# RWKV stage of a two-layer block: the routing's last step and the row transfers behind the third group instead of the fourth

## The reference

```python
xk = x * time_mix_k + x_prev * (1.0 - time_mix_k)      # same for xv, xr
k = xk @ W_k.T; v = xv @ W_v.T; r = sigmoid(xr @ W_r.T)
y = r * wkv_scan(k, v, decay, first)                   # over 2048 tokens, per channel
attn = y @ W_o.T

router_probs = softmax(x @ router)                     # 8 experts
topk_probs, topk_idx = top_k(router_probs, 2)
routed = sum over the two experts of topk_probs * expert(x)
ffn = routed + shared_expert(x)
```

## Time and profile before

| | us |
|---|---|
| median of 3 runs | 1508.13 (1507.18 to 1508.47) |
| the profiled execution, its own time | 1510.13 |
| its span | 1508.4 |
| RWKV stage in it | 1106.7 to 1295.8 |
| MoE stage in it | 1295.8 to 1508.4 |
| VectorE busy in 1109 to 1295.8 | 161.1 of 186.8 |
| TensorE busy there | 134.5 |
| ScalarE busy there | 119.2 |
| GpSimd busy there | 69.6 |

### The profile page before, as it was taken

How to read it: one execution, slowest core, us unless ns; L and a number is a source line. 1 busy time by engine, 2 the same in 40 slices (tenths; PEclk the granted TensorE clock), 3 DMA queues, 4 the chain that set the end, 5 groups by cost and what they waited for, 6 DMA issues and landing times. The chain is left out here.

```text
span 1508.4 us, 27417 instructions
## 1 busy us (share of the span) xinstructions
PE 1316.8 (87%) x9558; PEld 596.6 (40%) x9558; DVE 1272.9 (84%) x2268; ACT 998.8 (66%) x1316; POOL 324.4 (22%) x574
## 2 busy tenths in 40 slices
PE   4776999999999999999999986999767767689987
PEld 2454223232232332323322212766633334377754
DVE  6896999999999999999999933799868999665668
ACT  3452355888888888888888886666358665356642
POOL 3220000110102111020110202323100177300475
PEclk9897688999999999999999998999979889899999
DMA  6887312141423404242043024596372155686776
GB/s 206 269 257 219 57 33 45 20 81 29 83 46 41 85 7 79 46 79 49 11 76 74 12 48 116 169 315 198 136 232 86 56 171 184 215 253 205 229 227 194
DMA packets 158521, 186.16 MB, mean 123 GB/s; under 512 B 18228, under 2 KB 134708, under 8 KB 157364
## 3 DMA queue, kind: packets, MB, share of 16 engines
q1 hardware_dynamic: 135384, 151.45, 37.6%
q0 software_dynamic: 6144, 16.79, 3.6%
q10 hardware_dynamic: 16864, 16.26, 3.1%
HBM read 100.81 MB, written 83.36 MB: 122 GB/s over the span
## 5 line engine op out<-in xcount | busy, mean ns | idle before, releaser
L1334 DVE TENSOR_REDUCE att_m_part<-att_mx 128x1 f32<-128x512 f32 (+3 forms) x1152 | 680.8, 653 | 30.1 <-PE att_mx L1402 14.2
L1364 ACT ACTIVATE att_prob<-att_score,late_score_scale 128x1024 f32<-128x1024 f32 (+3 forms) x640 | 595.1, 986 | 167.2 <-PE att_score L1441 165.1
L1402 PE MATMUL att_mx<-early_kop,early_qop 48*128 48x512 f16 (+3 forms) x1280 | 354.6, 367 | 22.8 <-DVE att_m_part L1334 5.6
L1424 PE MATMUL att_pv<-att_prob,early_v 128*32 128x512 f32 (+3 forms) x2560 | 305.6, 550 | 2.0 <-POOL att_prob L1301 2.0
L1441 PE MATMUL att_score<-early_qop,early_kop 50*128 50x512 f16 (+3 forms) x1280 | 253.4, 358 | 10.3 <-ACT att_prob L1364 9.3
L1301 POOL TENSOR_SCALAR_AFFINE_SELECT att_prob<-att_prob 128x256 f32<-128x256 f32 x256 | 102.7, 406 | 671.4 <-ACT att_prob L1364 670.6
L1402 PEld LDWEIGHTS att_mx<-early_kop,early_qop 48*128 48x128 f16 x1280 | 98.5, 94 | 374.4 <-DVE att_m_part L1334 347.0
L2241 PE MATMUL rwkv_prod<-rwkv_xm,late_mixT 128*128 128x512 f32 x192 | 100.3, 675 | 37.1 <-ACT rwkv_kvr L2195 27.4
L1441 PEld LDWEIGHTS att_score<-early_qop,early_kop 50*128 50x128 f16 x1280 | 72.1, 94 | 72.5 <-ACT att_prob L1364 56.4
L1990 POOL DMA_INDIRECT rows<-rwkv_xs,routing_slot_i x64 | 69.6, 1087 | 112.2 <-DVE routing_slot_i L2082 93.0
L2462 POOL DMA_INDIRECT moe_yg<-results,routing_slot_i x64 | 64.6, 1009 | 128.6 <-issue 126.1
(11 more groups left out here) (264 smaller groups left out, 1752.9 us busy)
## 6 DMA issues: line engine op xcount, KB each, us to landing
va<-qkv_v SPq DMA_DIRECT2D x8, 1024.0 KB, 6.7
early_v<-va SPq DMA_DIRECT2D x8, 1024.0 KB, 7.5
moe_xt<-rows SPq DMA_DIRECT2D x30, 256.0 KB, 3.7
rows<-att_zeros SPq DMA_DIRECT2D x8, 928.0 KB, 6.5
early_kop<-qk SPq DMA_DIRECT2D x48, 128.0 KB, 4.4
routing_xp<-parts SPq DMA_DIRECT2D x24, 256.0 KB, 3.7
results<-moe_y ACTq DMA_DIRECT2D x24, 256.0 KB, 2.9
results<-blend_x ACTq DMA_DIRECT2D x22, 256.0 KB, 2.7
```

The lines of the kernel that those rows point to most:

```text
L1334: nc.vector.tensor_reduce(cells[:, sides[0]:sides[-1] + 1, some], mx[:, banks[0]:banks[-1] + 1, 0:len(hps) * w].rearrange("p a (h w) -> p ...
L1364: nc.scalar.activation(prob[:, r % (PROBS * HP), :, n0:], score[:, r % 2, :, n0:], ACT.Exp, scale=late_weights.score_scale[:, 0:1])\
L1402: op = nc.tensor.matmul(bank[:, n * w:(n + 1) * w], qop[rows, slot, t, hp, i * P:(i + 1) * P], kop[rows, slot, hp, c * GT:c * GT + w], sta ...
L1424: op = nc.tensor.matmul(pv[at, n0:], v[:, slot, j, at], prob[:, (st * HP + h // 2) % (PROBS * HP), h % 2, n0:], start=(j == 0), stop=(j == ...
```

## The change

The constant ROUTED of the RWKV stage goes from 4 to 3. It stands in the steps of VectorE, ScalarE, TensorE and SyncE, so all that is tied to it is done one step sooner: `below_top` in step 1, `choice`, the exponential and the count in step 2, `places` in step 3, the loads of chunks 2 and 3, 4 and 5, 6 and 7 in steps 5, 6 and 7. GpSimd's program is the same; its transfers wait for `places`.

```diff
@@ -1827,7 +1827,7 @@
     HALVES = TG * C // GT
     XP = 2
     CHUNKS = NT // TG
-    ROUTED = 4
+    ROUTED = 3
     wT, mix, unmix = late_weights.mixT, late_weights.mix, late_weights.unmix
```

## The result

The changed kernel takes 1513.65 us (median of 7 runs, 1512.43 to 1517.39) where the kernel before takes 1510.13 (7 runs, 1507.18 to 1510.70): ratio 1.0034, 95% interval 1.0021 to 1.0047, which is some 5.1 us slower (0.0034 of 1510). The ratio rests on all runs: the two medians alone lie 3.5 us apart, the two means 5.0. A second set of runs gave 1.0031 (1.0017 to 1.0046). The forecast was 8.9 us slower, 1517.0, range 1511 to 1523, with 0.85 on "slower by over 0.2%". The size is in the range; the sum is 3.8 us too high.

The account below looks back on a forecast made before the run. GpSimd's drain was taken to hold the barrier before the MoE stage. VectorE's end moves +10.2 and +4.6, +14.8 in all; with about 6 us gained at the barrier that is +8.9: 1517.0 us, range 1511 to 1523.

Parts of the forecast that it names:

- The frame: At the barrier before the MoE stage: GpSimd's drain opens it now; after the change VectorE comes last.
- rival C: At the barrier: GpSimd's drain is not hidden and stays behind VectorE's end, so the whole 14.8 us shows: 1522.9; 12 in 100.
- the sum without it: At VectorE's end in the RWKV stage, without the gain at the barrier: +14.8 us.
- The first term: VectorE in step 1: below_top waits for all eight groups of logits, done at 1143.0; +10.2 us on VectorE's path.
- so they stay where they are: TensorE's last logits: nothing ahead of them depends on the blends that come later, so they still end at 1142.97.
- 10.2 above: Upper bound on VectorE's wait for the logits; the lower was nothing, if the logits came by 1132.8.
- The second term: SyncE's queue: x 6 and x 7 go behind chunk loads, VectorE idles 8.4 us in place of 3.8; +4.6 us.
- The third term: At the barrier: GpSimd's drain ends before VectorE and no longer holds it; about -6 us.
- A: VectorE's wait: logits ready in time, so the barrier opens 5.9 us sooner, 1502.2; 4 in 100.
- B: Wait for the logits paid, x 6 and x 7 loaded in time: barrier opens 0.5 us later, 1508.6; 10 in 100.
- D: SBUF port shared by GpSimd and VectorE: VectorE pays for contention with the transfers, about 1 us more, 1518.0; 2 in 100.

Follow-up runs that it names:

- both edits together: Changed kernel with below_top moved to step 2 behind state 1 and the loads of chunks 2 to 7 in their old steps: 1497.45 us, 0.9936 against the kernel before.
- below_top alone: Kernel before (ROUTED = 4) with only below_top moved from step 2 to step 1: ratio 1.0048 (1.0034 to 1.0061).
- the edit for A's wait: Changed kernel with below_top moved from step 1 to step 2, behind state 1: ratio 0.9976 (0.9963 to 0.9990) against the kernel before.
- that for B's loads: Changed kernel with SyncE's loads of chunks 2 to 7 back in steps 6 to 8: ratio 0.9998 (0.9985 to 1.0011) against the kernel before.
- third profile of the changed kernel: Changed kernel profiled once more with no edit: logits ended 35.1 us behind the stage's start, the stage's end 160.0 us behind them.

## Why the prediction was right, and where its sizes were off

**The frame** held. It read GpSimd's drain, hidden in the queue's rows, as what opened the barrier, and VectorE's end as what would come next; rival C (the drain stays behind VectorE, 1522.9) and the sum without it are refuted by the barrier rows of the changed kernel and of both edits together.

**The first term**, below_top's wait, was set at +10.2 from logits that end at 36.3 us in the stage. In the changed kernel's profile they ended at 34.1 and the term was +8.1. The missing 2.1 are mostly TensorE's clock: the eight matmuls of 5.37 us took 3.67, and x 2 landed 0.5 sooner against the stage's start. In the other three profiles of this kernel the term was +11.9, +9.1 and +8.4, by where VectorE reached line 2024. The step that failed here is "so they stay where they are": true of the dependences, not of the clock, and one profile of before had shown one value of something that moves between executions. My upper bound ("10.2 above, as the wait is read off to a tenth of a us") was too narrow for the same reason. Measured as a change of its own (below_top alone), it is +7.2 (5.1 to 9.2). The range of 1511 to 1523 held the error, but it had been drawn for the landing of the loads and GpSimd's pace, with no room left for TensorE's clock, so here it held by luck.

**The second term**, the late loads, was mis-sized: +4.6 forecast, +2.5 in the first profile, +2.6 to +3.5 in the other three. The places were right: three idle times in states 5, 6 and 7, behind x 6 and x 7 that stand behind chunks. The sizes forecast were 2.0, 4.4 and 2.0, measured 2.45, 2.23 and 1.66. The middle one is the error, and its parts add up: x 7 sent 0.7 sooner against the slots, 1.0 less to land (5.46 in place of 6.48), and 0.45 that VectorE had already lost in the gap before. The 10.55 us from ScalarE's take of x to VectorE's state came out exact both times (1220.62 to 1231.17, 1240.79 to 1251.34).

**The third term**, -5.9 at the barrier, was right to 0.1 us.

So in the first profile two terms were 2.1 us too high each and the stage's +4.6 stood against a forecast of +8.9. That profile is the most favourable one: against the same profile of before, the stage is longer by 9.7, 5.9 and 5.5 us in the other three.

**The rivals.** A (logits ready in time) and B (loads in time) did not occur, but both are real kernels now: the edit for A's wait gives 3.6 us under the kernel before with the loads still late, that for B's loads gives no change, and both together 9.7 under. D, VectorE paying for the shared port: VectorE's steps beside the transfers are 17.86 us in the changed kernel too (1188.94 to 1206.80), as in the earlier trace rows, and a transfer of 1.95 us, right behind the start of VectorE's line 2124, comes in five of its groups (in four before). From GpSimd's timeline of the changed kernel:

```profile
1198.16 1.95 POOL L1990 DMA_INDIRECT rows<-rwkv_xs,routing_slot_i  x1 [0.30 <-issue]
...
1204.28 0.96 POOL L1990 DMA_INDIRECT rows<-rwkv_xs,routing_slot_i  x1 [0.30 <-issue]
```

The first begins 0.09 us behind VectorE's line 2124 (1198.07), the second 0.12 us ahead of its line 2137 (1204.40), which has two SBUF inputs as well. The Trainium skill, GPSIMD Engine Reference, section Specifications, says that GpSimd shares its SBUF interfaces with VectorE and that they contend with VectorE instructions that have two SBUF inputs. The trace agrees for GpSimd only beside line 2124 and not beside line 2137, and no run here shows a cost on VectorE.

## What to carry to other kernels

Moving work ahead by one step moves its waits and its queue neighbours with it: look where the operand of the moved work is complete, and what stands behind each moved DMA on its queue. Here the idea was sound and worth 9.7 us, but one constant tied the part that should move (choice, places) to two that should not (the first use of the logits, the chunks' loads). At a barrier, read the drains of the queues before the engines' last instructions: an engine with 64 transfers behind it may hold the next stage by 5 us after its work is done, and shortening any other engine buys nothing until that is cleared.

## What the runs showed that I had not expected

A wait placed right behind TensorE passes on its clock. Behind idle times of 2.8 to 3.6 us the same eight matmuls took 3.67 us at full clock, 5.37 at a granted 0.68, or 6.46 at 0.56, in different executions, and the changed kernel had both ends, at idle times of 3.00 and 3.25. The length of the idle time does not decide it: 5.37 us stands behind 2.79 us of it (the chunks' loads in their old steps), 3.67 behind 3.31 (the third profile of the changed kernel). What does is not shown. The kernel before had 7.7 us between the logits' end and VectorE's use of them (36.3 and 44.0 behind the stage's start) and did not feel it; the changed kernel has none. It does not make the changed kernel's times spread more, though: 15 runs of it lie within 7.8 us, 25 of the kernel before on one chip within 8.4, so other stages vary as much.

GpSimd's drain behind its transfers took 5.295 us in all twelve profiles of the seven kernels, ahead of the barrier by 14 us or last at it. Nothing in which these runs differ changed it. In each of them the same 64 transfers stood before it, the last of them issued 2.6 to 3.3 us before it began; whether the drain would be shorter with fewer of them, and what it consists of, was not tried.
